# Rotary projections and causal attention in one block, with the attention ordered by batch, and the sum of the rotated products of the second batch on GpSimd

## What is computed

```
def _L0_attn_b_ref(x, Wq, Wk, Wv, Wo):
    ...
    q, k, v = (proj(Wq), proj(Wk), proj(Wv))
    cos, sin = _rope_cache(T, hd, x.dtype)
    q = q * cos + _rotate_half(q) * sin
    k = k * cos + _rotate_half(k) * sin
    att = jnp.einsum('bhqd,bhkd->bhqk', q, k) / math.sqrt(hd)
    mask = jnp.triu(jnp.full((T, T), -jnp.inf, dtype=att.dtype), k=1)
    att = jax.nn.softmax(att + mask, axis=-1)
    out = jnp.einsum('bhqk,bhkd->bhqd', att, v)
    out = out.transpose(0, 2, 1, 3).reshape(B, T, D)
    return out @ Wo.T
...
x = x + _L0_attn_a_ref(_layernorm(x, axis=-1), ...)
x = x + _L0_ffn_ref(_layernorm(x, axis=-1), ...)
x = x + _L0_attn_b_ref(_layernorm(x, axis=-1), ...)
x = x + _L0_ffn_ref(_layernorm(x, axis=-1), ...)
```

## Time and profile before

| | us |
|---|---|
| median of three runs | 1193.61 (1193.3 to 1194.77) |
| the profiled execution | 1192.3 |
| its span in the trace | 1190.4 |
| PE busy | 1114.4 (94%) |
| DVE busy | 617.2 (52%) |
| ACT busy | 617.7 (52%) |
| GpSimd busy | 484.0 (41%) |
| mean granted TensorE clock | 0.974 |

### The profile page before, as it was taken

One profiled execution on the slowest core, in us unless ns is written; L12 is line 12 of the kernel. 1 busy time (PEld: TensorE's weight loads), 2 busy tenths in 40 slices (PEclk: granted clock), 3 DMA queues, 4 the chain that ended last, 5 costly groups with the idle time before them and its releaser, 6 DMA issues. The chain is left out here.

```text
span 1190.4 us, 33294 instructions
## 1 busy us (share of the span) xinstructions
PE 1114.4 (94%) x14272; PEld 858.3 (72%) x14272; DVE 617.2 (52%) x1362; ACT 617.7 (52%) x1163; POOL 484.0 (41%) x513
## 2 busy tenths in 40 slices
PE   4999999999999999999998898966899999998898
PEld 3888888888888888888887687852344444434777
DVE  5243434333343535454537545866777777742642
ACT  3543434444444545454546755431477666775662
POOL 1454454444454545555545475003122222221355
PEclk9999999999999999999999999985899999998999
DMA  3100101001010011020041100265022222000001
GB/s 123 53 2 3 53 3 46 9 2 60 2 47 16 22 66 36 16 79 16 21 146 60 40 1 10 80 192 104 2 55 54 55 55 56 2 1 1 1 18 53
DMA packets 15950, 49.58 MB, mean 42 GB/s; under 512 B 2432, under 2 KB 7104, under 8 KB 13120
## 3 DMA queue, kind: packets, MB, share of 16 engines
q1 hardware_dynamic: 15808, 47.50, 13.7%
HBM read 36.54 MB, written 10.75 MB: 40 GB/s over the span
## 5 line engine op out<-in xcount | busy, mean ns | idle before, releaser
L1638 DVE TENSOR_REDUCE ca_mx<-ca_S 128x1 f32<-128x640 f32 (+1 forms) x192 | 177.7, 955 | 55.2 <-PE ca_S L1508 52.4
L1603 ACT ACTIVATE ca_PT<-ca_ST 128x512 f32<-128x512 f32 (+1 forms) x304 | 159.1, 578 | 82.8 <-PE ca_ST L1532 79.8
L486 DVE SCALAR_TENSOR_TENSOR la_y<-la_g,la_O 128x512 f32<-128x512 f32 x64 | 41.1, 684 | 222.7 <-PE la_O L664 222.7
L576 PE MATMUL la_R<-a_hTh,WF 128*128 128x512 f32 x384 | 130.8, 405 | 3.7 <-ACT la_k L335 3.7
L1479 POOL TENSOR_SCALAR_AFFINE_SELECT ca_PT<-ca_PT 128x256 f32<-128x256 f32 (+1 forms) x112 | 48.6, 439 | 195.0 <-ACT ca_PT L1603 194.7
L288 POOL TENSOR_TENSOR la_yl<-la_y,la_yh 128x512 fp32r<-128x512 f32 x62 | 79.0, 1296 | 90.3 <-ACT la_yh L365 90.3
L275 POOL TENSOR_TENSOR la_qd<-q,la_C 128x512 f32<-128x512 f32 x64 | 80.8, 1283 | 84.6 <-PE la_O L664 80.8
L493 DVE TENSOR_TENSOR X<-la_R,X 128x512 f32<-128x512 f32 x64 | 44.3, 692 | 121.5 <-PE la_R L576 121.4
L330 ACT ACTIVATE la_v<-la_R 128x512 f32<-128x512 f32 x64 | 38.3, 598 | 113.8 <-PE la_R L576 113.8
L985 POOL TENSOR_TENSOR f_fl<-f_f,f_fh 128x512 fp32r<-128x512 f32 x48 | 61.6, 1296 | 87.4 <-ACT f_fh L877 87.4
L337 ACT ACTIVATE q<-la_R 128x512 f32<-128x512 f32 x64 | 38.3, 598 | 102.5 <-PE la_R L576 102.5
(11 more groups left out here) (218 smaller groups left out, 2878.8 us busy)
## 6 DMA issues: line engine op xcount, KB each, us to landing
la_Wraw<-w_quads_dram SPq DMA_DIRECT2D x7, 1280.0 KB, 6.6
q_parts<-rp_QP SPq DMA_DIRECT2D x4, 768.0 KB, 3.8
k_parts<-rp_KP SPq DMA_DIRECT2D x4, 768.0 KB, 3.5
ca_KS<-k_parts SPq DMA_DIRECT2D x10, 256.0 KB, 6.7
qw_w<-w_ffn_dram SPq DMA_DIRECT2D x12, 192.0 KB, 2.4
q_ffn<-qw_w SPq DMA_DIRECT2D x12, 192.0 KB, 1.9
X<-hidden_dram SPq DMA_DIRECT2D x4, 512.0 KB, 7.0
q<-hidden_dram SPq DMA_DIRECT2D x4, 512.0 KB, 5.1
```

Source lines behind the costliest of these rows:

```text
L576: m = pe.matmul(out, a, b, start=n == 0, stop=n == len(pairs) - 1)
L1603: act.activation(PT[:, (NM2 * g + b) % NPT, h:h + nh, 0:w], ST[at % NB][:, 0:nh * w].rearrange("p (h q) -> p h q", h=nh), ACT.Exp, scale=S ...
L1638: dve.reduce_max(out, src, AXX).then_inc(s1_free, 1)
```

## The change

1. The two blocks become one (`attention`); the end of the block between them is gone. The attention's tiles are allocated with the projections', and the banks are shared: the projections' Q and S banks are `ST0`, `ST1`, `ST2` and `OB`, and V's and the turned activations' are halves of `S10` and `S11`.
2. The groups go by batch: group g is head group g % 4 of batch g // 4. So groups 0 to 3 need batch 0 alone. SP loads the stacks of groups 0 and 1 after the four stores of batch 0, and those of group 2 behind the first maxima.
3. `V_AT` is (3, 4, 5, 6, 7, 8, 9, 10) in place of (3, 4, 6, 7, 9, 10, 12, 13).
4. In steps 12 to 15 PE's program has two segments of group 0's first pass behind the step's matmuls, and DVE's has their maxima at the end of the step; `N_AHEAD` is 16, and the maxima of the first half are turned behind segment 9.
5. The sum of the two products is GpSimd's in steps 8 to 15.
6. The mask is loaded at the block's start and cast by ACT, not DVE. ACT computes one exponential ahead of the second pass, which loads its table. The parts of batch 1 overwrite those of batch 0 (ACT waits for the stores). The rows of ones in the stacks are set earlier, with half as many elements of twice the size.
7. At the start of the kernel: ACT loads the table of the square root ahead of the data, by one square root of its own. DVE's order is moments 0, normalise 0, moments 1, moments 2, low 0, moments 3, normalise 1 to 3, low 1. PE projects k between the turns of block 0 and 1. ACT evicts k and q ahead of the split of the V weights. GpSimd waits for normalise 0 ahead of its first operation.

```
-    hg, b = g // 2, g % 2
+    hg, b = g % NG, g // NG
...
-        V_AT = (3, 4, 6, 7, 9, 10, 12, 13)
+        V_AT = (3, 4, 5, 6, 7, 8, 9, 10)
+        A_AT, A_EACH = 12, 2
...
-        N_AHEAD = reach(0, -1)
-        ENDS = [[reach(g, n) for n in range(NST)] for g in range(NG2)]
+        N_AHEAD = 2 * HALF[0]
+        ENDS = [[max(N_AHEAD, reach(g, n)) for n in range(NST)] for g in range(NG2)]
...
         def _(sp):
...
                 if n == NS // 2 + 1:
-                    sp.wait_ge(out_ok, 16 * NS // 4)
-                    gather_stacks(sp, 0, stacks0[:, 0], stacks0[:, 1], q_parts, k_parts, s_in0)
+                    for i in range(4):
+                        sp.wait_ge(out_ok[i], 16)
+                    sp.wait_ge(l_ok, 1)
+                    ln["turned"](sp)
+                    load(0)
+                    load(1)
...
+            rows(0, 0)
+            sp.wait_ge(m_ok, 2 * NS)
+            sp.wait_ge(vb_ok, NT // 2)
+            load(2)
...
         def _(pool):
...
+            for n in range(NS // 2, NS):
+                pool.wait_ge(m_ok, 2 * n + 2)
+                pool.tensor_tensor(t1[:, n % RS, :], t1[:, n % RS, :], t2[:], ALU.add).then_inc(a_ok, 1)
+            parts(0, 0)
...
         def _(pe):
...
                 if n in V_AT:
-                    values(V_AT.index(n))
+                    projected(V_AT.index(n))
+                if n == A_AT:
+                    pe.wait_ge(mk_ok, 1)
+                if n >= A_AT:
+                    for k in range(A_EACH * (n - A_AT), A_EACH * (n - A_AT + 1)):
+                        pass1(0, k)
+            for k in range(HALF[0], N_AHEAD):
+                if k == HALF[0] + 2:
+                    pe.wait_ge(m_ok, 2 * NS)
+                    rows(0, 0)
                 pass1(k // NSEG, k % NSEG)
-            rows(0, 0)
-            pe.wait_ge(one_ok, NSL)
+            pe.wait_ge(one_ok, 2)
...
         def _(dve):
...
-                if n < NS:
+                if n < NS // 2:
                     dve.wait_ge(m_ok, 2 * n + 2)
                     dve.tensor_tensor(t1[:, n % RS, :], t1[:, n % RS, :], t2[:], ALU.add).then_inc(a_ok, 1)
...
+                if A_AT <= n < NS:
+                    for k in range(A_EACH * (n - A_AT), A_EACH * (n - A_AT + 1)):
+                        pass1(0, k)
+            for k in range(HALF[0], N_AHEAD):
                 pass1(k // NSEG, k % NSEG)
```

More of the change, by code:

```diff
@@ L88, in moments, with table @@
             dve.bn_aggr(mv[:, t, :], stats[:, t, :]).then_inc(mv_ok, 1)
+    def table(act):
+        act.wait_ge(eps_ok, 1)
+        act.activation(root[:], epst[:], ACT.Sqrt, bias=epst[:])
     def deviation(act, b):
@@ L145, in ready, with turned @@
         pe.wait_ge(lo_ok, KT * (b + 1))
-    return {"sync": sync, "moments": moments, "deviation": deviation, "normalise": normalise, "shift": shift,
+    def turned(engine):
+        engine.wait_ge(t_ok, KT * NTB)
+    return {"sync": sync, "moments": moments, "table": table if norm else None,
+            "deviation": deviation if norm else None, "normalise": normalise, "shift": shift,
             "scaled": scaled, "turn": turn,
-            "high": high, "low": low, "ready": ready, "h_ok": h_ok if norm else None}
+            "high": high, "low": low, "ready": ready, "turned": turned, "h_ok": h_ok if norm else None}
 def linear_attention(nc, ctx, X, ident, ident_in, hTh, hTl, hidden, w_quads, c_quads, ln2, fin, q, WF, w_ffn, q_ffn, small):
@@ L746, in _ @@
             ln["turn"](pe, 0)
+            ln["ready"](pe, 0)
+            for n in range(2):
+                project(0, 0, "k", n)
             ln["turn"](pe, 1)
[L748 to L752 removed]
+            for n in range(2):
+                pe.wait_ge(silu_ok, n + 1)
+                project(0, 0, "q", n)
             ln["turn"](pe, 2)
@@ L1492, in _, with projected @@
         def _(pe):
+            def projected(n):
+                if n == 0:
+                    pe.wait_ge(rot.l_ok, 3)
+                if n >= 2:
+                    pe.wait_ge(ve_ok, n - 1)
+                for j in range(2):
+                    t = 2 * n + j
+                    for kt in range(KT):
+                        hi, lo = (h[:, kt, t * P:(t + 1) * P] for h in (hTh, hTl))
+                        a, c = (w[:, NV + kt * HID:NV + (kt + 1) * HID] for w in (Wh, Wl))
+                        o = VB[n % 2][:, j * HID:(j + 1) * HID]
+                        pe.matmul(o, hi, a, start=kt == 0, stop=False)
+                        pe.matmul(o, hi, c, start=False, stop=False)
+                        m = pe.matmul(o, lo, a, start=False, stop=kt == KT - 1)
+                m.then_inc(vb_ok, 1)
             def pass1(g, s):
@@ L1557, in back @@
                 ins.then_inc(s1_ok, 1)
-            pe.wait_ge(mk_ok, 1)
-            for k in range(N_AHEAD):
+            pe.wait_ge(rot.l_ok, 1)
+            for n, (dst, x, mt, tb) in enumerate(steps):
+                if n == 4:
+                    pe.wait_ge(rot.l_ok, 2)
+                ln["ready"](pe, tb)
+                if n >= 2:
+                    pe.wait_ge(m_ok, 2 * (n - 1))
+                for s, bank in ((x, QB[n % 2]), (x + 1, SB_[n % 2])):
+                    for kt in range(KT):
+                        hi, lo = (h[:, kt, tb * TB:(tb + 1) * TB] for h in (hTh, hTl))
+                        a, c = col(Wh, kt, s, mt), col(Wl, kt, s, mt)
+                        pe.matmul(bank[:], a, hi, start=kt == 0, stop=False)
+                        pe.matmul(bank[:], a, lo, start=False, stop=False)
+                        m = pe.matmul(bank[:], c, hi, start=False, stop=kt == KT - 1)
+                m.then_inc(p_ok, 1)
+                if n == 1:
+                    ln["turn"](pe, 2, H=H, banks=T)
+                if n == 4:
+                    ln["turn"](pe, 3, H=H, banks=T)
+                if n in V_AT:
+                    projected(V_AT.index(n))
[8 more added lines that the diff above has]
+                    rows(0, 0)
                 pass1(k // NSEG, k % NSEG)
-            rows(0, 0)
-            pe.wait_ge(one_ok, NSL)
+            pe.wait_ge(one_ok, 2)
             for g in range(NG2):
```

375 lines of the change are left out of this document (169 added, 206 removed).

## The result

The changed kernel takes **1186.06 us** (median of seven runs, 1184.06 to 1189.21), the kernel before 1193.3 (median of seven, 1191.48 to 1194.77). The ratio is 0.9945, 95% interval 0.9931 to 0.9959: **6.6 us faster** (4.9 to 8.2), half of the 13.2 that I had forecast. The profiled execution took 1187.56 us, its span is 1185.8, the mean granted clock 0.978.

What follows compares the result with a forecast made beforehand. PE, busy 94%, was taken as the bound, its one long hole between projections and attention. 9.5 us there (13.3 - 1.5 - 2.3) plus 3.7 at the start made 13.2 off 1192.3: 1180 us forecast, range 1171 to 1188.

Steps and rivals of the forecast that it cites:

- the middle: Projections and the attention's run-up: 9.5 us gained, from 13.3 less 1.5 for the clock and 2.3 for GpSimd's sum.
- Part 1: End of the projections: load issued 1.8 us later, PE stalls 4.5 us for the stack, projections end 8.6 us later.
- The clock: Step 13 behind the stall: PE at the lower clock costs 1.5 us, between 0 and 2.8.
- GpSimd's sum: Steps 13 to 15 and behind: GpSimd's SBUF access can hold up DVE's operations, costing 2.3 us, between 0 and 5.2.
- The run-up: From the last subtraction (806.4) to segment 16 (816.0, before 829.3), rows of maxima hidden: 13.3 us gained before costs.
- Part 3: Start of the kernel: V starts at 25.8 to 27.8 in place of 30.71, 3.7 us gained, low bound 2.5.
- Full clock in the run-up: Rival: PE stays at the upper clock before the second pass, no loss to GpSimd's port: 1172 us, chance 0.24.
- Two loads sharing the engines: Rival: group 1's load runs beside group 0's, the first stack lands up to 9 us later: 1190 us, chance 0.12.
- Slower than before: Rival: batch 1's projections wait for a stack delayed by shared loads and stores: 1200 us, chance 0.04.
- Late rows: Case: a 3.5 us store ahead of the rows of maxima delays the second pass: 1182 us, within the forecast's 0.55.
- GpSimd in the way each time: Rival: GpSimd's sum blocks DVE every time, the whole 5.2 us lost: 1183 us, within the forecast's 0.55.

Runs made afterwards that it cites:

- experiment 5: Changed kernel with no segments among the projection steps and the old V_AT: 1174.06 us with the sum on DVE, 1175.5 us with it on GpSimd.
- experiment 4: Changed kernel with 20 more matmuls ahead of the first segment, keeping PE busy in the stall: 1183.12 us, ratio 0.9926 to the kernel before.
- experiment 2: Changed kernel with the sum of the two products on DVE in all sixteen steps: 1183.28 us, ratio 0.9910 to the kernel before.
- experiment 6: Matmuls into an unread bank in the run-up, added to the kernel without segments among the projections and with DVE's sum: 1169.86 us.

## Why the prediction was right in its sign and wrong in its sum

The sign held, but the gain is half of the 13.2 us, and these were made up wrongly: the middle brought 1.4 us by the runs (4.0 at segment 16 of the trace) in place of 9.5, the start 5 to 6 in place of 3.7. That 1186.06 lies inside 1171 to 1188 owes something to luck: the start's surplus made up for a part of what the middle lacked.

**Part 1, the stack of group 0, is the step that failed.** I had the load issued 1.8 us later than before; it was 4.5. Of that, 2.8 are the two V pairs, as counted, and the 0.4 that DVE was late before did come off. What the sum lacked: PE waited 1.05 us ahead of step 9 for ACT to evict V (the row of 759.77), since V pairs now stand behind each of eight steps, and lost 0.4 more in gaps too short for the view to name. And where I took 0.6 off for one operation less, GpSimd's sum made DVE's way from step 9 to the issue of the load 0.7 longer (7.3 in place of 6.6). Then I put the landing 9.5 us behind the first issue and it was 10.7: all seven transfers count, and the last is issued 2.7 us behind the first and takes up to 7.8. My own bounds for it were 9.3 to 10.5; I took a value near the lower one, and it came out beyond the upper. Together 3.8 us: the first segment at 55.0 and not 51.2. I had seen the mechanism (a stall behind step 12, of 4.5 us; it was 6.05) and even named it as what makes all of batch 1 wait; I had not asked what the kernel would be without it. That is the larger lesson: experiment 5 removes the interleaving (and the new places of the V pairs), and has segment 16 9.4 us sooner with DVE's sum, 8.5 with GpSimd's. In my own sum the projections ended 8.6 us later than before in exchange for eight maxima of 6.6 us; the exchange was a loss on paper already.

**The clock, 1.5 us (bounds 0 to 2.8), was 2.6** (experiment 4). The stall made PE slow in nearly all of step 13.

**GpSimd's sum, 2.3 us (0 to 5.2), was 1.9 at segment 16, 2.8 by the medians and 4.1 by the ratios** (experiment 2). The size was near, the reason not: I took a middle between "always" and "never gets in", and it is always, eight times in eight, at 1.1 us instead of 1.3. Only steps 13 to 15 lie on the path. Against my plan, in which DVE's sum was gone at no cost, that is 3 x 1.1 = 3.3, and 2.7 of it show: DVE took 17.5 us from its first product of step 13 to the last subtraction instead of 14.8. Against the kernel with DVE's own sum it is less, 3 x (1.1 - 0.6) = 1.5, and the load's 0.5. The Trainium skill (SBUF — State Buffer, "Who interferes with whom") states that of such a pair the one that starts first locks the other out for its whole length; the trace agrees, with 1.75 to 1.79 us in place of 0.69.

At segment 16 the three misses make 3.8 + 1.1 + 0.4 (the stack; 2.6 less 1.5; 2.7 less 2.3), which is the 5.5 us between 82.9 and 88.4 but for 0.2.

**The run-up, from the last subtraction to segment 16, was right:** 9.7 us against 9.6. The rows of maxima had cover, as said: PE reaches the second pass without a wait, so neither the table load nor the cast delayed it. The period of the later groups is unchanged.

**Part 3, the start, was right at its own mark and too small in the total.** I said V at 27 and 3.7 us. Nine traces with the new start have V at 26.2 to 28.5, mean 27.0; three with the old one 30.7 to 31.4, mean 31.1: 4.1 us. By executions it is 6.3 (3.9 to 8.6) in the old kernel and 5.2 in the changed one (ratios; 5.5 by the medians). What lies between 4.1 and these is within the intervals. In the old kernel a part of it is the clock in the run-up, which rose earlier (2.5 us in the trace, and a mean clock of 0.977 over six executions where the kernel before has 0.973); in the changed one nothing shows where it lies.

**The rivals.** Full clock in the run-up: false here, 0.50 from 811 to 840; but its price of 4 us was good, since experiment 6 gets 4.2. Two loads sharing the engines: false, the seven transfers land as before. Slower than before: false; its decisive point, the stack later than 801.3, was never near. Late rows: not binding, PE didn't wait for them. GpSimd in the way each time: true in its mechanism, at about half of its 5.2.

## What to carry to other kernels

An instruction that waits for a transfer should not stand in an in-order queue ahead of work that is ready: count what the queue behind it loses, on both engines, and compare with the plain order, work first and the waiting part behind it. Moving an operation to an idle engine is a gain only if the two don't share a port with what runs next; read the neighbour's duration, not the moved one's. And when two parts of a change can be run apart, run them apart: here the start, last in the list of the change, brought most of the gain.
